# A fused two-block transformer kernel on one core: first group by sequences, last group by halves, and two biases moved from VectorE to TensorE

## The chip, the cores and the metric

The kernel runs on one core of a Trainium2 chip. The time is the device time of one launch in microseconds (us), the median of several runs. TensorE (PE) multiplies matrices into banks of the accumulation memory (2 KB for each of 128 partitions, so 512 float32 columns); VectorE (DVE) and ScalarE (ACT) read those banks, GpSimd (POOL) works on SBUF only, and SyncE (SP) issues the transfers. PEld is the loading of TensorE's weights.

## The reference

The input is 8 sequences of 256 tokens with 128 channels. Four parts follow each other, each with a residual and a layer norm behind it:

```python
# 1: linear attention: a decaying state for each of 16 heads of 8 channels
k = sigmoid(x @ key_w.T + key_b);  v, q = split(x @ vq_w.T)
kv = scan over t of (state * k + (1 - k) * v)            # 8 x 8 per head
x = layernorm(x + einsum(q, kv) @ out_w.T + out_b)
# 2: one of 8 linear maps, chosen by an argmax over noisy logits
x = layernorm(x + x @ W[idx] + b[idx])
# 3: attention without softmax through a symmetric metric per head
x = layernorm(x + nudged(x) @ mixer_w.T + mixer_b)
# 4: gated MLP, width 512, two more hidden layers with gelu
h = silu(x @ w1.T * s1) * (x @ w2.T * s2)
h = gelu(h @ h1.T * h1s);  h = gelu(h @ h2.T * h2s)
x = layernorm(x + h @ w3.T * s3)
```

## The kernel before, in words

The 8 sequences are handled in 4 groups (`NG`) of 2, so a group is `T` = 512 tokens, four tiles of 128 (`NT`). All groups run as one software pipeline: while group 2 is in part 1, group 1 is in part 3 and group 0 in part 4. There is no scheduler at run time. Each engine has a list of calls written out by hand (`without_weights` and `with_weights` for TensorE, plain lists for the others), executes it strictly in that order, and waits on semaphores where a call needs another engine's result. So what stands ahead of a call in its list matters as much as what it waits for.

*Part 1 of a group `a`.* `project(n)` makes key, value and query (three 512-column matmuls in float32). ScalarE moves them out (`projected`). VectorE takes the differences of the values (`value_steps`), ScalarE rounds them to the fast format fp32r (`high_values`, "high"), VectorE computes what the rounding lost (`low_values`, "low"), and `replicate(a, e)`, with e from 0 to 7, spreads them over the partitions with the matrix `rep_r`, which `cast_rows` makes at the start from a constant of the `heads` pack. VectorE then scans (`scan(a, e)`, two instructions of 256 columns), multiplies with the query (`read_state`), and TensorE applies the output weights (`attend(a, e)`).

*Parts 2 and 3.* `transposes(b, n)` turns the normed tiles, ScalarE moves them to SBUF (`move_x1`, `move_x2`, `high_x3`), `routed` multiplies with the chosen map plus identity into bank b4; `heads_of`, `gram_of`, `mix`, `through_metric` and `metric_out` do part 3 in b4 and b5. A norm is five calls: `norm_sum` adds the bias or residual and writes SBUF, `norm_stats`, `norm_moments` and `norm_varied` follow on VectorE, GpSimd raises the variance to the power -1/2 (`inverse_std`), and `norm_out` scales four tiles. For parts 2 and 3 `norm_sum` adds `chosen_b` or `mixer_b`.

*Part 4.* `gate_of` and `up_of`, two hidden layers (`hidden(c, layer, m)`, 8 matmuls each, high and low parts by the same fp32r weights), `narrow(c)` and `turn_back(c)`. ScalarE computes each gelu twice, rounded (`high_gelu`) and whole (`whole_gelu`); GpSimd or VectorE subtracts the two (`low_gelu`). `with_weights` begins once a flag has been computed and read by a branch.

## Time and profile before

| what | value |
|---|---|
| median of 3 runs (lowest, highest) | 204.92 us (204.56, 205.01) |
| the profiled execution's own time | 203.15 us |
| its span | 201.4 us |
| PE busy, instructions | 177.6 us (88%), 940 |
| DVE busy | 149.0 us (74%), 388 |
| ACT busy | 117.4 us (58%) |
| POOL busy | 68.4 us (34%) |
| mean granted TensorE clock | 0.989 |

The span is the part of the execution that the profiler sees; 1.75 us of the profiled execution lie around it. The profiled execution is 0.9% below the median of the runs shown. A row counts an engine as busy while an instruction is in it, so neighbouring instructions overlap a little; the distance between two starts says more about what one costs in a stream.

### The profile page before, as it was taken

Reading aid. Unit: us, or ns where it says so; the run is one execution under the profiler, and the core shown is the slowest. Engines: PE = TensorE matmul, PEld = TensorE weight load, DVE = VectorE, ACT = ScalarE, POOL = GpSimd, SP = SyncE. Lnnn points to the kernel's source line nnn. Section 1 sums busy time; section 2 is a strip of 40 time slices with the busy share of each in tenths; the row PEclk is TensorE's granted clock in tenths of the full one; section 3 lists DMA queues with packets and bytes.
Section 4 is the critical chain, followed back from the end, with each engine's and each line's share of the span. In section 5 each row is a group of like instructions: output and inputs, shape, how many; then the busy total and the mean of one; then the engine's idle time right before and its main releaser. Section 6 shows DMA issues by size and latency. Waiting matters only on the chain.

```text
span 201.4 us, 2831 instructions
## 1 busy us (share of the span) xinstructions
PE 177.6 (88%) x940; PEld 137.7 (68%) x940; DVE 149.0 (74%) x388; ACT 117.4 (58%) x178; POOL 68.4 (34%) x60
## 2 busy tenths in 40 slices
PE   7886878788976999999999999999899899999930
PEld 7245566466864887998789889866678677586810
DVE  0299999999999999999999955756772255753143
ACT  2698544095501785525577753498786459975720
POOL 4020002402012335343705545152549670554401
PEclk9999999999999999999999999999999999999995
DMA  5995002100000000010000000000001010000101
GB/s 144 333 433 215 3 0 80 52 0 0 3 0 0 3 3 0 0 52 3 0 2 0 3 0 0 0 0 3 0 0 37 19 52 3 2 0 1 51 3 55
DMA packets 6273, 7.83 MB, mean 39 GB/s; under 512 B 497, under 2 KB 5105, under 8 KB 6001
## 3 DMA queue, kind: packets, MB, share of 16 engines
q1 hardware_dynamic: 6256, 7.63, 11.1%
q8 instruction: 9, 0.15, 0.3%
q14 instruction: 8, 0.06, 0.1%
HBM read 6.58 MB, written 1.05 MB: 38 GB/s over the span
## 4 chain that ended last, share of the span: by engine, by line
PE 54%; DVE 23%; issue 10%; ACT 7%; DMA 2%; POOL 2%; POOLq 1%; DVEq 0%; SPq 0%; ACTq 0%
PE c_bank L1199 30%; DVE state L731 8%; PE y_bank L1106 7%; PE b_bank L1134 4%; PE b_bank L1129 3%; DVE read L741 3%; DMA heads_pack<-heads 2%; DVE stats L774 2%; PE rep_bank L1094 2%; PE b_bank L1199 2%; PE sum_bank L1199 2%; PE b_bank L1160 1%; DVE normed_lent L759 1%; DVE normed_lent L801 1%; ACT hid_even_high L482 1%
## 5 line engine op out<-in xcount | busy, mean ns | idle before, releaser
L731 DVE TENSOR_TENSOR_SCAN state<-rep_bank,keep 128x256 f32<-128x256 f32 x64 | 40.4, 675 | 2.3 <-PE rep_bank L1094 2.1
L1106 PEld LDWEIGHTS y_bank<-attend_pack,read 128*128 128x128 f32 x256 | 31.9, 191 | 8.2 <-DVE read L741 4.7
L1106 PE MATMUL y_bank<-attend_pack,read 128*128 128x128 f32 x256 | 33.6, 277 | 3.2 <-DVE total L766 1.9
L292 POOL TENSOR_TENSOR rstd<-varied,power 128x4 f32<-128x4 f32 x16 | 18.5, 1158 | 42.9 <-DVE varied L788 42.8
L741 DVE TENSOR_TENSOR read<-state,query 128x512 f32<-128x512 f32 x32 | 23.0, 730 | 0.5
L301 POOL TENSOR_TENSOR hid_odd_low<-hid,hid_odd_high 128x512 fp32r<-128x512 f32 x12 | 16.3, 1364 | 16.7 <-ACT hid L493 16.7
L493 ACT ACTIVATE hid<-c_bank,scales_pack 128x512 f32<-128x512 f32 x32 | 21.6, 683 | 0.0
L487 ACT ACTIVATE hid_even_high<-c_bank,scales_pack 128x512 fp32r<-128x512 f32 x16 | 11.0, 688 | 17.5 <-PE c_bank L1199 17.3
L1199 PE MATMUL c_bank<-hid_even_high,hidden_rounded 128*128 128x512 f32 x64 | 19.4, 410 | 1.0 <-ACT hid_even_high L482 0.8
L1199 PE MATMUL c_bank<-hid_odd_high,hidden_rounded 128*128 128x512 f32 x64 | 19.1, 410 | 0.0
L1199 PE MATMUL c_bank<-hid_odd_low,hidden_rounded 128*128 128x512 f32 x64 | 18.5, 398 | 0.4 <-DVE hid_odd_low L835 0.4
L1199 PE MATMUL c_bank<-hid_even_low,hidden_rounded 128*128 128x512 f32 x64 | 18.7, 400 | 0.0
L296 POOL TENSOR_TENSOR hid_even_low<-hid,hid_even_high 128x512 fp32r<-128x512 f32 x8 | 10.7, 1357 | 21.6 <-ACT hid_even_high L482 21.6
L301 POOL TENSOR_TENSOR hid_even_low<-hid,hid_even_high 128x512 fp32r<-128x512 f32 x8 | 10.8, 1355 | 16.3 <-ACT hid L493 16.3
L487 ACT ACTIVATE hid_odd_high<-c_bank,scales_pack 128x512 fp32r<-128x512 f32 x16 | 11.0, 688 | 8.2 <-PE c_bank L1199 8.1
L1199 PEld LDWEIGHTS c_bank<-hid_even_high,hidden_rounded 128*128 128x128 f32 x64 | 11.5, 189 | 4.6 <-ACT hid_even_high L482 1.7
L1199 PEld LDWEIGHTS c_bank<-hid_odd_low,hidden_rounded 128*128 128x128 f32 x64 | 12.0, 187 | 3.9 <-DVE hid_odd_low L835 0.7
L1199 PEld LDWEIGHTS c_bank<-hid_even_low,hidden_rounded 128*128 128x128 f32 x64 | 12.0, 188 | 3.7 <-DVE hid_even_low L830 1.1
L1071 PE MATMUL c_bank<-xT_lent,project_pack 128*128 128x512 f32 x24 | 12.7, 621 | 0.8 <-ACT keep L392 0.6
L1199 PEld LDWEIGHTS c_bank<-hid_odd_high,hidden_rounded 128*128 128x128 f32 x64 | 11.6, 190 | 2.2
L482 ACT CAST hid_even_high<-hid 128x512 fp32r<-128x512 f32 x16 | 9.9, 618 | 2.7 <-DVE hid L825 2.5
L801 DVE TENSOR_SCALAR normed_lent<-normed_lent,moments,rstd 128x128 f32<-128x128 f32 x32 | 8.9, 340 | 3.5 <-POOL rstd L292 3.4
(133 smaller groups left out, 336.6 us busy)
## 6 DMA issues: line engine op xcount, KB each, us to landing
hidden_pack<-hidden SPq DMA_DIRECT2D x2, 1024.0 KB, 11.0
xT_lent<-x_chan SPq DMA_DIRECT2D x4, 256.0 KB, 5.7
xt<-x_tok SPq DMA_DIRECT2D x4, 256.0 KB, 2.8
mlp_pack<-mlp SPq DMA_DIRECT2D x1, 768.0 KB, 8.0
out<-xT_lent SPq DMA_DIRECT2D x3, 256.0 KB, 2.3
attend_pack<-attend SPq DMA_DIRECT2D x1, 640.0 KB, 5.1
metric_pack<-metric SPq DMA_DIRECT2D x1, 448.0 KB, 12.5
out<-xT_lent SPq DMA_DIRECT2D x2, 128.0 KB, 1.8
```

What stands on the lines that cost most here:

```text
L292: nc.gpsimd.tensor_tensor(rstd[n][:], varied[n][:], power[:], ALU.pow).then_inc(ln_rstd[n], 1)
L296: nc.gpsimd.tensor_tensor(hid_parts[0][1][:, m, :], hid[:, m, :], hid_parts[0][0][:, m, :].bitcast(F32), ALU.subtract).then_inc(low_pool[0 ...
L301: nc.gpsimd.tensor_tensor(hid_parts[layer][1][:, m, :], hid[:, m, :], hid_parts[layer][0][:, m, :].bitcast(F32), ALU.subtract).then_inc(lo ...
L482: nc.scalar.copy(hid_parts[0][0][:, m, :], hid[:, m, :]).then_inc(product_high, 1)
L487: nc.scalar.activation(hid_parts[layer][0][:, m, :], c_bank[m % 2][:], ACT.Gelu, scale=scale).then_inc(gelu_high, 1)
L493: nc.scalar.activation(hid[:, m, :], c_bank[m % 2][:], ACT.Gelu, scale=scale).then_inc(gelu_done, 1)
L731: ins = nc.vector.tensor_tensor_scan(state[:, e % STATES, at], rep_bank[e % 2][:, at], keep[:, a * T + s * SEQ:a * T + (s + 1) * SEQ], 0.0 ...
L741: nc.vector.tensor_tensor(read[:, e % READS, :], state[:, e % STATES, :], query[:, a * T:(a + 1) * T], ALU.mult).then_inc(read_ready, 1)
L801: nc.vector.tensor_scalar(normed[n][:, tile(j)], total[n][:, tile(j)], moments[n][:, j, 0:1], rstd[n][:, j:j + 1], ALU.subtract, ALU.mult) ...
L1071: nc.tensor.matmul(proj_bank[n % 2][:], (key_w_sb, value_w_sb, query_w_sb)[k], xT[:, g * T:(g + 1) * T], start=True, stop=True).then_inc(p ...
L1106: ins = nc.tensor.matmul(y1_bank[:, tile(j)], read[:, e % READS, tile(j)], out_w_rep_sb[:, e, :], start=(e == 0 and j == 0), stop=False, s ...
L1199: return nc.tensor.matmul(bank_[:], weights[exact[0]][k], moving, start=(k == 0 and i == 0), stop=(k == last and i == 1))
```

## The change

Four things are done together.

1. *First group by sequences.* The packs `project` and `heads` are cut in four, the first 256 columns of the channel-major input come on their own, and three more transfers stand ahead of the input of groups 1 to 3. The first group's value and key projections, value differences, high and low parts and the first scan run for each sequence of 256 columns apart (`first_*`). Only 2 of the 8 slices of `rep_r` are cast at first. The warm-up is 6 matmuls instead of 8.
2. *Biases by TensorE.* `with_bias` puts behind each of the four tile products of `routed` and `metric_out` a second matmul into the same columns: a constant of 1/32 (64 x 128) times the bias in high and low part (64 x 128, fp32r). `norm_sum` is gone for parts 2 and 3, and their norms read bank b5 directly, `norm_stats` and `norm_out` alike. So `routed` goes from b4 to b5, and the small products between change banks too; `up_of(c, 0)`, which writes b5, now waits for `norm_out` of part 3 and no longer for its `norm_sum`.
3. *Last group's end by halves.* The last gelu, low part, `narrow`, scaling, turning back and norm of group 3 are done for tokens 0 to 255 and 256 to 511 apart (`*_last`, `narrow_early`, `narrow_late`).
4. *Other orders.* The lists of all engines are in a new order throughout.

```diff
-    ("project", (("key_w", P), ("value_w", P), ("query_w", P), ("key_b", 1))),
-    ("heads", (("rows_of", HD * HEADS), ("head_sum", P))),
+    ("values", (("value_w", P),)),
+    ("keys", (("key_w", P), ("query_w", P), ("key_b", 1))),
+    ("rows", (("rows_of", HD * HEADS),)),
+    ("sums", (("head_sum", P),)),
...
+        total[1] = total[2] = b5_bank
...
-            load_pack("project")
-            for g in range(NG):
+            load_pack("values")
+            sp.dma_start(xT[:, 0:SEQ], x_chan[:, 0:SEQ]).then_inc(x0_loaded, 16)
+            load_pack("keys")
+            sp.dma_start(xT[:, SEQ:T], x_chan[:, SEQ:T]).then_inc(xT_loaded[0], 16)
+            load_pack("rows")
+            load_pack("scales")
+            load_pack("sums")
+            load_pack("attend")
+            for g in range(1, NG):
                 at = slice(g * T, (g + 1) * T)
                 sp.dma_start(xT[:, at], x_chan[:, at]).then_inc(xT_loaded[g], 16)
-                if g == 0:
-                    load_pack("heads")
-                    load_pack("scales")
-                    load_pack("attend")
...
+            def cast_rows(i):
+                n = (0, 2, HD)[i], (0, 2, HD)[i + 1]
+                act.wait_ge(loaded["rows"], 16)
+                nc.scalar.copy(rep_r[:, n[0]:n[1], :].rearrange("p e (h d) -> p e h d", h=HEADS),
+                               rows_of_sb[:, n[0]:n[1], :].unsqueeze(3).to_broadcast([P, n[1] - n[0], HEADS, HD])
+                               ).then_inc(rep_cast, 1)
+
+            def first_value(s):
+                act.wait_ge(first["proj"], 2 * s + 1)
+                act.wait_ge(const_ready, 3)
+                nc.scalar.copy(value[:, s, 1:SEQ + 1], proj_bank[s][:, 0:SEQ]).then_inc(first["out"], 1)
+
+            def first_keep(s):
+                act.wait_ge(first["proj"], 2 * s + 2)
+                act.wait_ge(loaded["keys"], 16)
+                nc.scalar.activation(keep[:, s * SEQ:(s + 1) * SEQ], (b4_bank, b5_bank)[s][:, 0:SEQ], ACT.Sigmoid,
+                                     bias=key_b_sb).then_inc(first["out"], 1)
+
+            def first_query():
+                act.wait_ge(proj_ready, 1)
+                nc.scalar.copy(query[:, 0:T], y1_bank[:]).then_inc(proj_out, PROJECTIONS)
+
+            def first_high(s):
+                act.wait_ge(*((first["steps"], 1), (dv_whole, 1))[s])
+                nc.scalar.copy(dvalue_parts[0][0][half(0), s * SEQ:(s + 1) * SEQ],
+                               dvalue[half(0), s * SEQ:(s + 1) * SEQ]).then_inc((first["high"], dv_high)[s], 1)
...
+            def high_bias(n):
+                if n == 0:
+                    act.wait_ge(const_ready, 1)
+                    ins = nc.scalar.activation(thirty_seconds[:], ones[0:P // 2, :], ACT.Copy, scale=1.0 / 32.0)
+                elif n == 1:
+                    act.wait_ge(loaded["metric"], 16)
+                    ins = nc.scalar.copy(bias_parts[1][:], mixer_b_sb[0:P // 2, :])
+                else:
+                    act.wait_ge(chosen_loaded, 32)
+                    ins = nc.scalar.copy(bias_parts[0][:], chosen_b[0:P // 2, :])
+                ins.then_inc(bias_high, 1)
...
+            def high_gelu_last(i):
+                act.wait_ge(hidden_ready, 2 * NH * NG)
+                at = slice(i * T // 2, (i + 1) * T // 2)
+                nc.scalar.activation(hid_parts[2][0][:, NH - 1, at], c_bank[1][:, at], ACT.Gelu,
+                                     scale=h2s_sb[:, NH - 1:NH]).then_inc(last["gelu_high"], 1)
+
+            def whole_gelu_last(i):
+                act.wait_ge(hidden_ready, 2 * NH * NG)
+                at = slice(i * T // 2, (i + 1) * T // 2)
+                nc.scalar.activation(hid[:, NH - 1, at], c_bank[1][:, at], ACT.Gelu,
+                                     scale=h2s_sb[:, NH - 1:NH]).then_inc(last["gelu"], 1)
+
+            def narrow_out_last(i):
+                act.wait_ge(last["narrow"], i + 1)
+                nc.scalar.activation(narrowed[:, i * T // 2:(i + 1) * T // 2], (c_bank[0], rep_bank[0])[i][:, 0:T // 2],
+                                     ACT.Copy, scale=s3_sb[:, 0:1]).then_inc(last["narrow_out"], 1)
...
+            def first_steps(s):
+                dve.wait_ge(first["out"], 2 * s + 1)
+                nc.vector.tensor_tensor(dvalue[:, s * SEQ:(s + 1) * SEQ], value[:, s, 0:SEQ], value[:, s, 1:SEQ + 1],
+                                        ALU.subtract).then_inc((first["steps"], dv_whole)[s], 1)
+
+            def first_low(s):
+                dve.wait_ge(*((first["high"], 1), (dv_high, 1))[s])
+                at, parts = slice(s * SEQ, (s + 1) * SEQ), dvalue_parts[0][0]
+                nc.vector.tensor_tensor(parts[half(1), at], dvalue[half(0), at], parts[half(0), at].bitcast(F32),
+                                        ALU.subtract).then_inc((first["low"], dv_ready)[s], 1)
+
+            def first_scan(s):
+                dve.wait_ge(*((first["rep"], 1), (rep_ready, 1))[s])
+                dve.wait_ge(first["out"], 2 * s + 2)
+                at = slice(s * SEQ, (s + 1) * SEQ)
+                nc.vector.tensor_tensor_scan(state[:, 0, at], (sum_bank, rep_bank[0])[s][:, at], keep[:, at], 0.0, ALU.add,
+                                             ALU.mult).then_inc((first["scan"], scan_done)[s], 1)
...
-                if n in (1, 2):
-
-                    dve.wait_ge((routed_ready, metric_ready)[n - 1], g + 1)
-                    if n == 1 and g == 0:
-                        dve.wait_ge(chosen_loaded, 32)
-                    view = "p (j c) -> p j c"
-                    nc.vector.tensor_tensor(total[n].rearrange(view, j=NT),
-                                            (b4_bank, b5_bank)[n - 1][:].rearrange(view, j=NT),
-                                            (chosen_b[:], mixer_b_sb)[n - 1].unsqueeze(1).to_broadcast([P, NT, P]),
-                                            ALU.add).then_inc(ln_sum[n], 1)
-                else:
-                    dve.wait_ge(y1_ready if n == 0 else turned_back, g + 1)
-                    dve.wait_ge(res_ready[n], g + 1)
-                    nc.vector.tensor_tensor(total[n][:], y1_bank[:], (res0 if n == 0 else res3)[:],
-                                            ALU.add).then_inc(ln_sum[n], 1)
+                dve.wait_ge(y1_ready if n == 0 else turned_back, g + 1)
+                dve.wait_ge(res_ready[n], g + 1)
+                nc.vector.tensor_tensor(total[n][:], y1_bank[:], (res0 if n == 0 else res3)[:],
+                                        ALU.add).then_inc(ln_sum[n], 1)
 
             def norm_stats(n, g):
                 if g > 0:
                     dve.wait_ge(ln_moments[n], g)
-                dve.wait_ge(ln_sum[n], g + 1)
+
+                dve.wait_ge((ln_sum[0], routed_ready, metric_ready, ln_sum[3])[n], g + 1)
...
+            low_gelu(3, 2, 2)
+            low_gelu_last(0)
             norm_out(3, 2)
-            low_gelu(3, 2, 2)
-            low_gelu(3, 2, 3)
-            norm_sum(3, 3)
-            norm_stats(3, 3)
-            norm_moments(3, 3)
-            norm_varied(3, 3)
-            norm_out(3, 3)
+            low_gelu_last(1)
+            norm_sum_last(0)
+            norm_stats_last(0)
+            norm_moments_last(0)
+            norm_varied_last(0)
+            norm_sum_last(1)
+            norm_stats_last(1)
+            norm_moments_last(1)
+            norm_varied_last(1)
+            norm_out_last(0)
+            norm_out_last(1)
 
...
+            def first_project(k, s):
+                pe.wait_ge(loaded[("values", "keys")[k]], 16)
+                pe.wait_ge((x0_loaded, xT_loaded[0])[s], 16)
+                bank_ = proj_bank[s] if k == 0 else (b4_bank, b5_bank)[s]
+                nc.tensor.matmul(bank_[:, 0:SEQ], (value_w_sb, key_w_sb)[k], xT[:, s * SEQ:(s + 1) * SEQ], start=True,
+                                 stop=True).then_inc(first["proj"], 1)
+
+            def first_project_query():
+                pe.wait_ge(loaded["keys"], 16)
+                pe.wait_ge(x0_loaded, 16)
+                pe.wait_ge(xT_loaded[0], 16)
+                nc.tensor.matmul(y1_bank[:], query_w_sb, xT[:, 0:T], start=True, stop=True).then_inc(proj_ready, 1)
+
+            def first_replicate(s):
+                pe.wait_ge(*((first["low"], 1), (dv_ready, 1))[s])
+                pe.wait_ge(rep_cast, 1)
+                at = slice(s * SEQ, (s + 1) * SEQ)
+                nc.tensor.matmul((sum_bank, rep_bank[0])[s][:, at], rep_r[:, 0, :], dvalue_parts[0][0][:, at], start=True,
+                                 stop=True).then_inc((first["rep"], rep_ready)[s], 1)
...
+            def with_bias(src, w, bias):
+                for j in range(NT):
+                    nc.tensor.matmul(b5_bank[:, tile(j)], src[:, tile(j)], w(j), start=True, stop=False)
+                    ins = nc.tensor.matmul(b5_bank[:, tile(j)], thirty_seconds[:], bias[:], start=False, stop=True)
+                return ins
...
-                per_tile(b4_bank, x1T, lambda j: passed_w[:]).then_inc(routed_ready, 1)
-
-            def project_metric():
-                pe.wait_ge(loaded["metric"], 16)
-                nc.tensor.matmul(b5_bank[:, 0:P], metric_sb, proj_t_sb, start=True, stop=True).then_inc(pm_ready, 1)
-
-            def heads_of(b):
-                pe.wait_ge(x2_moved, b + 1)
                 if b == 0:
                     pe.wait_ge(pm_copied, 1)
                 else:
 
                     pe.wait_ge(product_done, NH * (b - 1) + 3)
+                with_bias(x1T, lambda j: passed_w[:], bias_parts[0]).then_inc(routed_ready, 1)
...
+                        ins = nc.tensor.matmul(b4_bank[:, tile(s)], heads[:, at], heads[:, at],
...
-                per_tile(b5_bank, x2T, lambda j: through[:, j // TPS, :]).then_inc(metric_ready, 1)
+                pe.wait_ge(mixed_moved, b + 1)
+                with_bias(x2T, lambda j: through[:, j // TPS, :], bias_parts[1]).then_inc(metric_ready, 1)
...
-                narrow(3)
-                turn_back(3)
+                narrow_early(0)
+                narrow_late(0)
+                narrow_early(1)
+                turn_back_last(0)
+                narrow_late(1)
+                turn_back_last(1)```

The start of ScalarE's list, first before, then after (the names are those of tiles; a number behind L is a line).

```order
2 L377 ACTIVATE spare<-ones 128x1 [waits const_ready]
3 L384 CAST rep_r<-heads_pack 128x1024 [waits heads_loaded]
4 L392 ACTIVATE keep<-c_bank,project_pack 128x512 [waits project_loaded,proj_ready]
5 L395 COPY value<-c_bank 128x2x256 [waits const_ready,proj_ready]
6 L406 CAST dvalue_first<-dvalue 64x512 [waits dv_whole]
```

```order
2 L398 ACTIVATE spare<-ones 128x1 [waits const_ready]
3 L406 CAST rep_r<-rows_pack 128x256 [waits rows_loaded]
4 L413 COPY value<-c_bank 128x256 [waits const_ready,first_proj]
5 L418 ACTIVATE keep<-b_bank,keys_pack 128x256 [waits keys_loaded,first_proj]
6 L413 COPY value<-c_bank 128x256 [waits const_ready,first_proj]
7 L427 CAST dvalue_first<-dvalue 64x256 [waits first_steps]
```

The cast of `rep_r` still stands first, but has a quarter of its columns; the value comes ahead of the key, by 256 columns.

TensorE's list around the branch that starts `with_weights`, before and after, with the numbers of the banks.

```order
60 L1094 MATMUL rep_bank0<-dvalue_first0,rep_r 128x512
61 L1106 MATMUL y1_bank<-attend_pack,read 128x128 x4
62 L1129 MATMUL b4_bank<-metric_pack,normed_lent 128x128 x4
63 L1094 MATMUL rep_bank1<-dvalue_first0,rep_r 128x512
64 L1485 TENSOR_LOAD fits_flag
```

```order
78 L1262 MATMUL rep_bank1<-dvalue_first0,rep_r 128x512
79 L1262 MATMUL rep_bank0<-dvalue_second0,rep_r 128x512
80 L1275 MATMUL y1_bank<-attend_pack,read 128x128 x4
81 L1299 MATMUL b4_bank<-metric_pack,normed_lent 128x128 x4
82 L1275 MATMUL y1_bank<-attend_pack,read 128x128 x4
83 L1713 TENSOR_LOAD fits_flag
```

One `replicate` (the fifth of group 2) and one `attend` more now stand ahead of the branch.

The end of VectorE's list after the change; before, `norm_out(3, 2)` stood ahead of the last two `low_gelu`, and the five calls of the last norm followed once, for 512 columns.

```order
277 L897 TENSOR_TENSOR hid_even_low<-hid,hid_even_high 128x256 [waits last_gelu]
278 L891 TENSOR_SCALAR xT_lent<-xT_lent,moments,rstd 128x128 [waits stored,ln3_rstd]
279 L891 TENSOR_SCALAR xT_lent<-xT_lent,moments,rstd 128x128 x3
280 L897 TENSOR_TENSOR hid_even_low<-hid,hid_even_high 128x256 [waits last_gelu]
281 L905 TENSOR_TENSOR xT_lent<-y_bank,res 128x256 [waits ln3_out,res3_ready,last_turned]
```

Four scalings of group 2 (numbers 278 and 279) now stand between the two halves of the last low part.

## Rows read from the trace of the kernel before

**Rows 1.** Windows: busy us and count of each engine, TensorE's clock, DMA share, GB/s.

```profile
12.37:64.65 52.28, 41.78 (x244) 30.43 (x244) 51.10 (x126) 25.36 (x37) 6.04 (x7) 1.00 0.15 56
64.65:129.00 64.35, 64.35 (x390) 55.80 (x391) 58.09 (x142) 36.37 (x58) 27.54 (x20) 1.00 0.02 5
129.00:193.02 64.02, 60.83 (x276) 45.09 (x274) 32.87 (x100) 48.17 (x74) 30.73 (x26) 1.00 0.04 13
```

**Rows 2.** Timeline of the start: start, us, engine, line, operation, idle before.

```profile
6.07 1.04 ACT L384 CAST rep_r<-heads_pack 128x1024 fp32r<-128x1024 f32 x1 [3.83 <-DMA heads_pack<-heads]
...
7.02 0.68 ACT L392 ACTIVATE keep<-c_bank,project_pack 128x512 f32<-128x512 f32 x1
7.60 0.58 ACT L395 COPY value<-c_bank 128x512 f32<-128x512 f32 x1
...
8.28 0.69 DVE L707 TENSOR_TENSOR dvalue<-value 128x512 f32<-128x512 f32 x1 [1.58 <-ACT value L395]
...
11.10 1.27 DVE L731 TENSOR_TENSOR_SCAN state<-rep_bank,keep 128x256 f32<-128x256 f32 x2
```

**Rows 3.** Timeline around the branch, VectorE and TensorE.

```profile
62.21 1.26 DVE L731 TENSOR_TENSOR_SCAN state<-rep_bank,keep 128x256 f32<-128x256 f32 x2
...
63.53 0.49 PE L1094 MATMUL rep_bank<-dvalue_first,rep_r 128*128 128x512 f32 x1 [0.91 <-DVE state L731]
64.65 0.47 PE L1199 MATMUL sum_bank<-x3T_high,mlp_rounded 128*128 128x512 f32 x1 [0.63 <-issue]
```

**Rows 4.** Chain that ended last: start us, us in the chain, what.

```profile
69.28 0.44 PE b_bank L1129 x4
...
71.07 0.89 PE b_bank L1134 x8
...
73.09 5.69 PE c_bank L1199 x24
```

**Rows 5.** Groups by form: busy us, mean ns; operations of VectorE and ScalarE.

```profile
L816 DVE TENSOR_TENSOR x3T_low<-b_bank,x3T_high 128x512 fp32r<-128x512 f32 x4 | 2.7, 682 | 1.0 <-ACT x3T_high L462 1.0
L835 DVE TENSOR_TENSOR hid_odd_low<-hid,hid_odd_high 128x512 fp32r<-128x512 f32 x4 | 2.8, 689 | 4.2 <-ACT hid L493 4.2
...
L455 ACT COPY mixed<-b_bank 128x256 f32<-128x256 f32 x4 | 1.5, 372 | 5.4 <-PE b_bank L1168 5.4
```

**Rows 6.** Chain that ended last, part 3's norm of group 3.

```profile
162.11 0.70 DVE normed_lent L759
...
164.55 1.02 POOL rstd L292
...
166.08 1.01 PE b_bank L1129 x4
```

**Rows 7.** Who waited for whom, TensorE, 64 to 192 us: total, times, longest.

```profile
PE c_bank L1199 <- ACT hid_even_high L482: 0.8, 2, 0.7
PE b_bank L1129 <- DVE normed_lent L801: 0.7, 2, 0.4
```

**Rows 8.** Timeline of the end.

```profile
190.46 0.69 ACT L487 ACTIVATE hid_even_high<-c_bank,scales_pack 128x512 fp32r<-128x512 f32 x1 [0.60 <-PE c_bank L1199]
...
192.50 0.50 PE L1199 MATMUL c_bank<-hid_even_low,mlp_rounded 128*128 128x512 f32 x1 [0.45 <-DVE hid_even_low L835]
193.03 0.69 ACT L497 ACTIVATE gate<-c_bank,scales_pack 128x512 f32<-128x512 f32 x1 [1.31 <-PE c_bank L1199]
...
193.77 0.66 PE L1278 MATMUL y_bank<-metric_pack,gate 128*128 128x128 f32 x4 [0.78 <-ACT gate L497]
194.53 0.69 DVE L766 TENSOR_TENSOR xT_lent<-y_bank,res 128x512 f32<-128x512 f32 x1 [2.08 <-PE y_bank L1278]
195.32 0.87 DVE L774 BATCH_NORM_STATS2 stats<-xT_lent 128x6 f32<-128x128 f32 x4
...
196.96 1.01 POOL L292 TENSOR_TENSOR rstd<-varied,power 128x4 f32<-128x4 f32 x1 [7.61 <-DVE varied L788]
198.00 1.11 DVE L801 TENSOR_SCALAR xT_lent<-xT_lent,moments,rstd 128x128 f32<-128x128 f32 x4 [1.12 <-POOL rstd L292]
```

More of the change, by code:

```diff
@@ L179, in build @@
         proj_ready, proj_out = sem("proj_ready"), sem("proj_out")
+        first = {name: sem("first_" + name) for name in ("proj", "out", "steps", "high", "low", "rep", "scan")}
+        last = {name: sem("last_" + name) for name in ("gelu_high", "gelu", "low", "narrow", "narrow_out", "turned", "sum",
+                                                       "stats", "moments", "varied", "rstd")}
         dv_whole, dv_high, dv_ready = sem("dv_whole"), sem("dv_high"), sem("dv_ready")
@@ L957, in _ @@
-            norm_sum(2, 1)
             norm_stats(2, 1)
@@ L1076, in sum_query @@
                 if a == 0:
-                    pe.wait_ge(loaded["heads"], 16)
+                    pe.wait_ge(loaded["sums"], 16)
+                    pe.wait_ge(first["scan"], 1)
                 else:
```

627 lines of the change are left out of this document (367 added, 260 removed).

## The prediction, made before the changed kernel was run

> **What bounds the kernel now.** I read the busy time by stretch first, then the chain that ended last, and the timeline where the chain changes engine. They give four stretches. To 12 us the kernel fills its pipeline. From 12.37 to 64.65 us VectorE is busy 51.1 of 52.3 us while TensorE has 10.5 us idle: VectorE's list sets the pace [rows 1]. The chain turns to TensorE at the branch: VectorE ends a scan at 63.47, the `replicate` that waited for it starts at 63.53, and the first product of part 4 at 64.65, with 0.63 us of branching ahead of it [rows 3]. From there to 129 us TensorE has no gap at all, and to 193.02 it idles 3.2 of 64.0 us [rows 1]. So there each matmul added or taken away counts in full. The last stretch is a serial hand-over from engine to engine, from the last gelu (190.46) to the last scaling (ends 199.11), with 2.3 us behind it for the store [rows 8].
>
> **The change, part by part.** Sums are made against the profiled execution (203.15 us); the median of the runs shown is 0.9% above it, and I scale at the end.
>
> *Start.* ScalarE waited until 6.07 us for the `heads` pack, cast 1024 columns in 1.04 us, then made the key and only then the value, which reached VectorE at 8.28; the first scan began at 11.10 [rows 2] and its second half ended at 12.37. After the change the pack of the rows is the fifth transfer, but the bytes up to and with it (columns of the packs and of the input, 512 bytes each) are 512 KB and were 576 KB, so I let it land at the same 6.1. A 256-column pass of ScalarE took 0.37 [rows 5]: cast to 6.5, value to 6.9, difference on VectorE (0.4, somewhat over half of 0.69) to 7.3. ScalarE meanwhile does key, second value and then the high part to 8.1; low part 8.5, `replicate` of 256 columns 8.9, first scan 9.6, `low_values(0, 1)` 10.3, second scan 10.95. That is 1.4 us earlier; with a dozen hand-overs I take 1.2, bounds 0.5 (the pack lands later, behind three more issues) and 1.8. Three more issues also shift SP's queue by some 1.3 us: group 1's input, tokens and MLP weights come later, but the first reader of each still stands behind VectorE's backlog. If that cover fails, the start's gain is what it costs. The warm-up's two missing matmuls cost nothing: TensorE waits for input then.
>
> *To the branch.* The new last item before it is `attend(2, 1)`, which needs `read_state(2, 1)`. Against the old point (the scan's end at 63.47) VectorE's list has more: one pair of scans, 1.26; one read, 0.69; two `low_bias`, 0.4 (128 columns, 0.22 each by the statistics [rows 8]). It has less: two `norm_sum` of parts 2 and 3, 1.4 at 0.70 [rows 6]; one `norm_stats`, 0.87 [rows 8], and one `direct_product`, 0.69 by rows of that shape [rows 5], which now follow. Net 0.6 less, with the start 1.8: VectorE is there at 61.7, `attend` takes 0.89, hand-over and branch 0.7, so 63.3 instead of 64.65. And TensorE has one `replicate` (0.49, [rows 3]) and one `attend` (0.89, as eight records of that size take in [rows 4]) behind it already, 1.4 more. Together 2.7; I take **-2.5**, since VectorE's own 1.2 us of gaps may grow. Bounds -0.5 and -3.5.
>
> *The bias matmuls.* 32 are added, 24 of them (six calls in groups 1 to 3) where TensorE is the bound. No row shows an fp32r matmul of 128 columns. The nearest: single-record matmuls of 128 columns (the transposes) stand 0.11 apart; the float32 product of that shape costs 0.22 (eight records, 0.89); an fp32r product of 512 columns costs 0.237 (5.69 for 24), a quarter of which is 0.06 [rows 4]. The weight load would hold the last one up, as it does in the transposes, so I take 0.11: **+2.7**, bounds +1.4 and +5.3. The eight calls of before the branch lie in TensorE's idle time there.
>
> *The norms from the bank.* On the chain part 3's norm of group 3 runs from 162.11 to 166.08, where the transposes start; 0.70 of it is `norm_sum` [rows 6]. TensorE has two hidden products to cover it and runs short; waits of this kind and idle around them make 0.7 us by the waits' own sum [rows 7] and part of the 3.2 us. A norm shorter by 0.7 stays under cover in groups 2 and 3: **-1.0**, bounds 0 and -2. What is late next there is ScalarE's rounding of the product (0.8 [rows 7]), which the change does not touch. Bank as source is no dearer in the trace: 682 ns against 689 from SBUF for the same shape [rows 5]. The statistics and scalings from a bank have no row; I take them as unchanged. The Trainium skill speaks against this (VectorE: DVE Perf Modes, "Why PSUM operands drop a tier"): a float32 operation with one source may run at double rate from SBUF but never from a bank. By that page's clock it would cost an estimated 0.07 us for each scaling of 128 columns, 0.27 a norm, and no row here shows such a scaling. The same mechanism, priced from rows, is a rival below. The later release for `up_of(c, 0)` costs nothing: the same norm must end before there is an x3 to multiply.
>
> *The end.* From 190.46: four gelu passes of 256 columns end at 190.85, 191.2, 191.5 and 191.9; low part 0 at 191.65, its last two matmuls 192.0, scaling 192.4. TensorE then does six 256-column matmuls of half 1 (192.7) and turns half 0 back (193.0). Half 1's low part stands behind `norm_out(3, 2)`, 1.11 as the same shape takes [rows 8]: 193.15 instead of 192.3; matmuls 193.5, scaling 193.9, turned 194.2. VectorE sums and measures half 0 to 194.4 and half 1 to 195.6; GpSimd's power took 1.01 for four columns [rows 8] and I keep that for two, to 196.7; the last two scalings end at 197.3 against 199.11. That is 1.8, and with eight hand-overs of 0.05 **-1.4**, bounds -0.7 and -2.0. The third store must have landed before half 0 is scaled; it starts near 193.4 and has until 195.6. Splitting six calls into narrower ones adds **+0.1**.
>
> *Sum.* -2.5 + 2.7 - 1.0 - 1.4 + 0.1 = -2.1: 201.05 us for a profiled execution, and times 204.92/203.15, **202.8 us**.
>
> **The rivals.**
> - *The narrow fp32r matmul is dear* (the side of slower). At 0.22, the price of the float32 product, six calls on TensorE's path cost 5.3: 203.15 + 0.5 = 203.7, or 205.5. It decides from about 0.19 us each on. For it: nothing in the trace shows that fp32r keeps its rate at 128 columns. Against: fp32r needs one record where float32 needs two. 17%.
> - *Scaling from the bank is slow.* A column costs VectorE 1.2 ns (0.69 for a sum of 512 less 0.22 for statistics of 128, over 384 [rows 8]); if half of 128 is lost, 0.3 a norm comes back on VectorE and on the norm's chain: two norms before the branch, 0.6, and 0.4 of cover, so 203.8. For it: no row of such a scaling. Against: [rows 5]. 10%.
> - *The start's gain does not arrive.* A pack late by a microsecond, or one of VectorE's new neighbours waiting, and only -0.5 of the 2.5 is left: 204.8 to 205.3. For it: VectorE has 1.2 us of slack in 52 [rows 1], so one badly placed wait shows at once. 13%.
> - *The orders fit better still.* TensorE's 3.2 us of idle time mostly gone and the bias at 0.06: 200.5 to 201.5. 12%.
> - The forecast, 202.0 to 203.8: 48%.
>
> **Numbers.** Forecast, good order and slow scaling are all faster (70%); a change within 0.2% (0.4 us, about what this kernel's runs can tell from none) comes from the third rival's near half and the edge of the first, 11%; slower 19%. The range reaches from the good orders to the dear matmul, 200.8 to 205.4.
>
> **What would show it.** In the changed profile: the first scan near 9.0 us; the first product of part 4 near 63.3 with one `attend` more behind it; bias matmuls 0.11 apart from their neighbours, a call of `routed` 1.3 us long and not 0.9 or 1.8; statistics at 0.22 and scalings at 0.28 distance from b5; no TensorE wait ahead of part 3's transposes; the last scaling's end 7.2 us behind the start of the last gelu and not 8.65. Wrong would make it: gaps on TensorE between 64 and 129 us, where there are none now, or a bias call near 1.8 us.

## Result and profile of the changed kernel

The changed kernel took **213.72 us** (median of four runs, 213.29 to 214.48) where the kernel before, on the same chip, took 204.96 (204.56 to 205.15): a ratio of **1.0434, interval 1.0399 to 1.0469**. Forecast were 202.8 us and a range up to 205.4. The change makes the kernel slower by 4%, outside the range and the other way from what was forecast. Runs of the kernel before fall into two groups: around 203.0 us at a mean granted clock of 0.985 to 0.99, as its profile (203.15 us), and around 204.6 us near 0.98, as the four runs here by their times. A few slow runs are left out of the ratios and medians below.

The profiled execution took 213.29 us, its span 211.5. I cut it at the marks of the prediction (times are those of the profiled executions; the last column reaches from the end of the last scaling to the execution's own time):

| kernel | first scan | first product of part 4 | from there to the last gelu | last gelu to last scaling's end | behind it |
|---|---|---|---|---|---|
| before | 11.10 | 64.65 | 125.81 | 8.65 | 4.04 |
| after | 8.25 | 64.83 | 135.90 | 7.02 | 5.54 |

The medians are 8.76 us apart, the two profiles 10.14. This difference is +0.18 to the branch, **+10.09** between it and the last gelu, -1.63 in the hand-over at the end, +1.50 behind the last scaling. The middle stretch in windows, from the first product of part 4 to the last gelu, of before and of after (columns as in [rows 1]):

```profile
64.65:190.46 125.81, 123.08 (x657) 99.77 (x658) 90.15 (x241) 83.28 (x130) 58.26 (x46) 1.00 0.03 9
```

```profile
64.83:200.73 135.90, 132.93 (x674) 104.34 (x674) 87.95 (x235) 84.38 (x132) 56.27 (x46) 1.00 0.02 7
```

TensorE idles 2.7 us in the one and 3.0 in the other, at the full clock in both. So waits don't make the +10.1: TensorE is *busy* 9.9 us longer. The timeline of TensorE in after, one call of `metric_out` with its eight matmuls (start, us, line, operation), shows on what:

```profile
134.79 0.39 PE L1309 MATMUL b_bank<-through,x1T 128*128 128x128 f32 x2
135.11 0.32 PE L1310 MATMUL b_bank<-bias_parts,thirty_seconds 64*128 64x128 f32 x1
135.36 0.49 PE L1309 MATMUL b_bank<-through,x1T 128*128 128x128 f32 x2
135.78 0.33 PE L1310 MATMUL b_bank<-bias_parts,thirty_seconds 64*128 64x128 f32 x1
...
137.12 0.32 PE L1310 MATMUL b_bank<-bias_parts,thirty_seconds 64*128 64x128 f32 x1
137.38 1.16 PE L1275 MATMUL y_bank<-attend_pack,read 128*128 128x128 f32 x8
```

A bias matmul has 64 rows of weights, a product 128; I call this number the height of the weights. From one bias matmul to the next it is 0.67 us, where a product alone has 0.22 (0.89 for the call of four in [rows 4]). A bias matmul costs 0.45 us, not 0.11, and only 0.25 of it (135.11 to 135.36) passes before the next product starts: the product behind it is dearer as well, 0.42 to the next bias matmul instead of 0.22. The forecast named a call of 1.8 us as the sign of being wrong; this one takes 2.59 (134.79 to 137.38). The weight loads of the same stretch show what goes with it:

```profile
135.11 0.18 PEld L1310 LDWEIGHTS b_bank<-bias_parts,thirty_seconds 64*128 64x128 f32 x1
135.36 0.30 PEld L1309 LDWEIGHTS b_bank<-through,x1T 128*128 128x128 f32 x2
135.78 0.18 PEld L1310 LDWEIGHTS b_bank<-bias_parts,thirty_seconds 64*128 64x128 f32 x1
```

Each load starts in the same hundredth as its own matmul. It isn't done under the matmul before it, and that at both changes of height, from 128 to 64 and back.

The start, in the timeline of after (compare [rows 2]):

```profile
5.28 0.40 ACT L406 CAST rep_r<-rows_pack 128x256 fp32r<-128x256 f32 x1 [3.04 <-DMA rows_pack<-rows]
...
6.04 0.42 DVE L783 TENSOR_TENSOR dvalue<-value 128x256 f32<-128x256 f32 x1 [6.04 <-ACT value L413]
...
8.25 0.69 DVE L796 TENSOR_TENSOR_SCAN state<-sum_bank,keep 128x256 f32<-128x256 f32 x1
```

The first scan is 2.85 us earlier, twice the forecast (7.71 to 8.72 us in the profiles of the variants with this start). The pack landed at 5.28 and not at 6.1, and from the end of the first high part (7.16) to the scan it took 1.09 us where I had counted 1.5. Up to 36 us stands a wait longer than any that TensorE has in the kernel before (1.8 us at most from 12 to 64 us), on GpSimd's and TensorE's timelines:

```profile
34.07 0.46 POOL L301 TENSOR_TENSOR passed_w<-chosen_w,metric_pack 128x128 f32<-128x128 f32 x1 [19.47 <-DMA chosen_b<-ffn_b]
34.48 1.02 POOL L307 TENSOR_TENSOR rstd<-varied,power 128x4 f32<-128x4 f32 x1
...
36.04 1.15 PE L1299 MATMUL b_bank<-metric_pack,normed 128*128 128x128 f32 x4 [3.40 <-DVE normed L891]
```

GpSimd's list has the chosen weights, which come with a late DMA, ahead of the first norm's power. TensorE stands 3.40 us for that norm, and its clock falls behind the wait (third column from the end, 30 to 40 us and 40 to 50 us):

```profile
30.00:40.00 10.00, 6.43 (x24) 4.09 (x24) 9.27 (x28) 4.25 (x8) 1.44 (x2) 0.83 0.13 39
40.00:50.00 10.00, 9.89 (x55) 7.13 (x56) 7.90 (x23) 2.27 (x5) 2.62 (x2) 1.00 0.09 26
```

From 40 us on TensorE is busy 9.89 of 10 us *ahead* of the branch. The eight bias matmuls of group 0, which I had put at nothing, lie between 39 and 59 us. The end, against [rows 8]:

```profile
200.73 0.47 ACT L552 ACTIVATE hid_even_high<-c_bank,scales_pack 128x256 fp32r<-128x256 f32 x1 [0.60 <-PE c_bank L1382]
...
205.01 0.70 POOL L336 TENSOR_TENSOR rstd<-varied,power 128x2 f32<-128x2 f32 x1 [5.02 <-DVE varied L926]
...
206.85 1.31 SPq L274 DMA_DIRECT2D out<-xT_lent  x2
207.15 0.60 DVE L933 TENSOR_SCALAR xT_lent<-xT_lent,moments,rstd 128x128 f32<-128x128 f32 x2 [0.33 <-POOL rstd L336]
```

Here the forecast of 7.2 us is met to 0.2: 7.02 from gelu to scaling. The power takes 0.70 for two columns, not 1.01, so without that luck it would have been 7.3.

### The profile page after: what moved, and what is told of

It reads as the page before. It is cut to its first block, busy times and chain, and to the rows that moved or that the text cites. A ratio compares the mean times of both kernels' runs of the same rounds, so it can differ in the third digit from the quotient of the medians.

```text
span 211.5 us, 2947 instructions
## 1 busy us (share of the span) xinstructions
PE 191.5 (91%) x981; PEld 146.9 (69%) x981; DVE 147.4 (70%) x387; ACT 118.4 (56%) x188; POOL 64.5 (31%) x61
## 3 DMA queue, kind: packets, MB, share of 16 engines
q1 hardware_dynamic: 6688, 7.63, 10.9%
HBM read 6.58 MB, written 1.05 MB: 36 GB/s over the span
## 4 chain that ended last, share of the span: by engine, by line
PE 71%; DVE 10%; issue 5%; ACT 4%; DMA 3%; SPq 2%; POOL 1%; POOLq 0%; DVEq 0%
PE c_bank L1382 32%; PE y_bank L1275 9%; PE b_bank L1309 6%; PE b_bank L1299 4%; PE b_bank L1310 4%; DVE state L831 3%; DMA xT_lent<-x_chan 3%; PE c_bank L1236 2%; PE rep_bank L1262 2%; PE b_bank L1382 2%; PE b_bank L1341 2%; PE b_bank L1304 2%; PE sum_bank L1382 2%; PE y_bank L1282 1%; DVE read L841 1%
## 5 line engine op out<-in xcount | busy, mean ns | idle before, releaser
L831 DVE TENSOR_TENSOR_SCAN state<-rep_bank,keep 128x256 f32<-128x256 f32 x62 | 38.9, 673 | 1.6 <-PE rep_bank L1262 1.6
L1275 PEld LDWEIGHTS y_bank<-attend_pack,read 128*128 128x128 f32 x256 | 31.9, 191 | 6.6 <-DVE read L841 3.3
L1275 PE MATMUL y_bank<-attend_pack,read 128*128 128x128 f32 x256 | 34.4, 279 | 1.2 <-DVE read L841 0.6
L307 POOL TENSOR_TENSOR rstd<-varied,power 128x4 f32<-128x4 f32 x15 | 15.9, 1060 | 56.9 <-DVE varied L878 56.8
L841 DVE TENSOR_TENSOR read<-state,query 128x512 f32<-128x512 f32 x32 | 22.6, 714 | 0.1
L541 ACT ACTIVATE hid_even_high<-c_bank,scales_pack 128x512 fp32r<-128x512 f32 x15 | 10.3, 689 | 16.9 <-PE c_bank L1382 16.8
L316 POOL TENSOR_TENSOR hid_odd_low<-hid,hid_odd_high 128x512 fp32r<-128x512 f32 x12 | 16.0, 1339 | 11.7 <-ACT hid L547 11.6
L1382 PE MATMUL c_bank<-hid_even_high,hidden_rounded 128*128 128x512 f32 x64 | 19.1, 410 | 0.3 <-ACT gate L530 0.3
L1382 PE MATMUL c_bank<-hid_odd_high,hidden_rounded 128*128 128x512 f32 x64 | 19.2, 411 | 0.0
L1382 PE MATMUL c_bank<-hid_odd_low,hidden_rounded 128*128 128x512 f32 x64 | 18.4, 397 | 0.5 <-DVE hid_odd_low L975 0.5
L1382 PE MATMUL c_bank<-hid_even_low,hidden_rounded 128*128 128x512 f32 x64 | 18.5, 398 | 0.0
L316 POOL TENSOR_TENSOR hid_even_low<-hid,hid_even_high 128x512 fp32r<-128x512 f32 x8 | 10.6, 1330 | 20.5 <-ACT hid L547 20.5
L864 DVE BATCH_NORM_STATS2 stats<-b_bank 128x6 f32<-128x128 f32 x32 | 7.1, 285 | 13.8 <-PE b_bank L1310 13.8
L1382 PEld LDWEIGHTS c_bank<-hid_odd_low,hidden_rounded 128*128 128x128 f32 x64 | 12.0, 188 | 3.8 <-DVE hid_odd_low L975 0.9
L1382 PEld LDWEIGHTS c_bank<-hid_even_low,hidden_rounded 128*128 128x128 f32 x64 | 12.0, 188 | 3.4 <-DVE hid_even_low L970 0.7
L311 POOL TENSOR_TENSOR hid_even_low<-hid,hid_even_high 128x512 fp32r<-128x512 f32 x8 | 10.4, 1323 | 12.5 <-ACT hid_even_high L536 12.5
L1382 PEld LDWEIGHTS c_bank<-hid_even_high,hidden_rounded 128*128 128x128 f32 x64 | 11.4, 189 | 3.4 <-ACT gate L530 0.7
L1382 PEld LDWEIGHTS c_bank<-hid_odd_high,hidden_rounded 128*128 128x128 f32 x64 | 11.5, 189 | 2.2
L891 DVE TENSOR_SCALAR normed_lent<-b_bank,moments,rstd 128x128 f32<-128x128 f32 x32 | 10.9, 403 | 2.7 <-POOL rstd L307 2.7
```

The lines of the kernel that those rows point to most:

```text
L307: nc.gpsimd.tensor_tensor(rstd[n][:], varied[n][:], power[:], ALU.pow).then_inc(ln_rstd[n], 1)
L311: nc.gpsimd.tensor_tensor(hid_parts[0][1][:, m, :], hid[:, m, :], hid_parts[0][0][:, m, :].bitcast(F32), ALU.subtract).then_inc(low_pool[0 ...
L316: nc.gpsimd.tensor_tensor(hid_parts[layer][1][:, m, :], hid[:, m, :], hid_parts[layer][0][:, m, :].bitcast(F32), ALU.subtract).then_inc(lo ...
L541: nc.scalar.activation(hid_parts[layer][0][:, m, :], c_bank[m % 2][:], ACT.Gelu, scale=scale).then_inc(gelu_high, 1)
L831: ins = nc.vector.tensor_tensor_scan(state[:, e % STATES, at], rep_bank[e % 2][:, at], keep[:, a * T + s * SEQ:a * T + (s + 1) * SEQ], 0.0 ...
L841: nc.vector.tensor_tensor(read[:, e % READS, :], state[:, e % STATES, :], query[:, a * T:(a + 1) * T], ALU.mult).then_inc(read_ready, 1)
```

## The experiments

All ratios are to the kernel before, run beside the variants on the same chip; its median there was 203.42 us for the a runs, 203.89 for b and c, 203.20 for d. The ratio need not be the quotient of the medians. Between runs with different letters the ratios say more than the times.

**a1: the changed kernel without the bias matmuls.** It leaves the biases of parts 2 and 3 out.

```diff
-                nc.tensor.matmul(b5_bank[:, tile(j)], src[:, tile(j)], w(j), start=True, stop=False)
-                ins = nc.tensor.matmul(b5_bank[:, tile(j)], thirty_seconds[:], bias[:], start=False, stop=True)
+                ins = nc.tensor.matmul(b5_bank[:, tile(j)], src[:, tile(j)], w(j), start=True, stop=True)
```

> The changed kernel with the 32 bias matmuls left out (so the biases of parts 2 and 3 are left out of the result). In the changed kernel a tile of a call with bias takes 0.67 us where the product alone took 0.22, so 0.45 more, 24 times on TensorE's path, and the operation behind each call another 0.2. If these matmuls are the cause of the loss, about 11 to 12 us go: 202 us. If the loss lies in the new orders or in the early stall at 33 us, it stays above 210.

Measured: 205.17 us, 1.0076 (1.0043 to 1.0108), not the 202 expected. The matmuls carry most of the loss: 3.6 of the 4.3% by the ratios, or 8.5 of the 8.8 us by the medians. But without them the kernel is still no faster than before, where my sum without its +2.7 gave -4.8.

**a2: the bias over 128 rows instead of 64.**

```diff
-        bias_parts = [sb(f"bias_parts{n}", [P // 2, P], F32R) for n in (1, 2)]
-        thirty_seconds = sb("thirty_seconds", [P // 2, P], F32R)
+        bias_parts = [sb(f"bias_parts{n}", [P, P], F32R) for n in (1, 2)]
+        thirty_seconds = sb("thirty_seconds", [P, P], F32R)
```

(with 1/64 in place of 1/32 and the low parts in rows 64 to 127).

> The changed kernel with bias matmuls over 128 rows instead of 64 (constant 1/64, bias high and low in 64 rows each); same count, same columns, same format. Theory S (the switch between 64 and 128 rows keeps weights from being loaded behind the running matmul): the tile falls from 0.67 to about 0.33, the loss shrinks by 8 us: 205 to 206 us. Rival N (an fp32r matmul of 128 columns is slow by itself, whatever its rows): no change, 213 to 214 us.

Measured: 205.43 us, 1.0109 (1.0037 to 1.0182). As many matmuls of as many columns, only the height of the weights changed, and 8.3 us are gone by the medians, 7.9 between the two profiles, 6.6 by the ratios. TensorE's timeline of a2:

```profile
91.51 0.30 PE L1310 MATMUL b_bank<-bias_parts,thirty_seconds 128*128 128x128 f32 x1
91.60 0.30 PEld L1309 LDWEIGHTS b_bank<-through,x1T 128*128 128x128 f32 x2
91.66 0.44 PE L1309 MATMUL b_bank<-through,x1T 128*128 128x128 f32 x2
...
91.85 0.31 PE L1310 MATMUL b_bank<-bias_parts,thirty_seconds 128*128 128x128 f32 x1
```

The period is 0.34 us, so 0.12 for a bias matmul, and the next product's load (91.60) starts under the running matmul (91.51 to 91.81). The windows from the branch to the last gelu agree, of a1 and of a2:

```profile
62.93:191.72 128.79, 122.97 (x650) 97.97 (x650) 88.60 (x235) 84.71 (x132) 56.13 (x46) 1.00 0.02 7
```

```profile
62.60:192.68 130.08, 125.55 (x674) 100.78 (x674) 88.62 (x235) 84.61 (x131) 56.10 (x46) 1.00 0.03 7
```

24 bias matmuls add (125.55 - 122.97) / 24 = **0.11 us** each over 128 rows, my price to the digit, and (132.93 - 122.97) / 24 = **0.42** each over 64. The Trainium skill (TensorE: Matmul & The Clock Gate, "Part 3: Packing small matmuls — row/col tiling") says that a weight load overlaps a running matmul only where their row groups (strips of 32 rows) differ; earlier in the same section it also lets a load go ahead into a background weight buffer. The loads over all 128 rows here do overlap (91.60 under 91.51 to 91.81), against the first statement and in line with the second. The loads at a change of height, 64 rows beside 128, don't.

**a3: one 64-row bias matmul of 512 columns ahead of the four products.**

```diff
+                nc.tensor.matmul(b5_bank[:].rearrange("p (j c) -> p j c", j=NT), thirty_seconds[:],
+                                 bias[:].unsqueeze(1).to_broadcast([bias.shape[0], NT, P]), start=True, stop=False)
                 for j in range(NT):
-                    nc.tensor.matmul(b5_bank[:, tile(j)], src[:, tile(j)], w(j), start=True, stop=False)
-                    ins = nc.tensor.matmul(b5_bank[:, tile(j)], thirty_seconds[:], bias[:], start=False, stop=True)
+                    ins = nc.tensor.matmul(b5_bank[:, tile(j)], src[:, tile(j)], w(j), start=False, stop=(j == NT - 1))
```

> The changed kernel with one 512-column bias matmul (64 rows, the bias repeated four times by its access pattern) ahead of the four products of a call instead of four of 128 columns. Theory S: one switch in and out instead of four, a call takes about 0.89 + 0.24 + 0.4 = 1.5 instead of 2.67: 7 us less, 206 to 207 us. Rival N: 0.24 for the wide one and nothing else, 1.13 a call: 9 us less, 204 to 205 us.

Measured: 207.42 us, 1.0152 (1.0076 to 1.0227). Two changes of height in a call instead of eight:

```profile
111.86 0.50 PE L1308 MATMUL b_bank<-bias_parts,thirty_seconds 64*128 64x512 f32 x1
112.29 1.16 PE L1311 MATMUL b_bank<-passed_w,x1T 128*128 128x128 f32 x8
...
113.28 0.39 PE L1275 MATMUL y_bank<-attend_pack,read 128*128 128x128 f32 x2
```

A call takes 1.42 us (111.86 to 113.28), 2.59 in after. Its wide matmul takes 0.43 us to the next start and its products 0.99; over 128 rows (d1 below) they take 0.32 and 0.89. So one pair of changes costs 0.2 us here, and 0.3 around each 128-column matmul in after. That it is the change of height that is dear and not a 64-row matmul by itself is my reading and not shown: a3 has fewer of both, and no variant has two 64-row matmuls in a row.

**a4: part 2 undone in the new orders.** VectorE adds the biases again, in eight `norm_sum`.

> The changed kernel with part 2 undone: VectorE adds the biases from bank b5 into SBUF in a norm_sum again (0.7 us each, 8 times), no bias matmuls; all orders, the start and the end as changed. If the bias matmuls are the whole loss: 202 to 203.5 us, at or under the kernel before (205). If the new orders cost by themselves: above 205.

Measured: 214.72 us, 1.0544 (1.0471 to 1.0617). TensorE's waits from 64 to 192 us of a4, and the same one in a1:

```profile
PE b_bank L1312 <- DVE normed_lent L898: 6.9, 8, 2.1
```

```profile
PE b_bank L1299 <- DVE normed_lent L891: 1.3, 1, 1.3
```

The new orders can't carry VectorE's eight sums; this variant also keeps the one bank and the later release of the change. Part of its time goes with the granted clock, 0.74 in 30 to 40 us and 0.94 in 100 to 130 (a1: 0.89 and 1.00). So the parts of the change aren't additive: in these orders part 2 is worth up to 9.6 us (a1 against a4), which a good form of it brings and the 64-row form spends again.

**b1: the kernel before with the end by halves alone.**

> The kernel before with part 3 alone: the end of group 3 by halves, all other lists as before. In the changed kernel the last scaling ends 7.0 us behind the start of the last gelu, before it was 8.65; but the span ran 3.75 us on behind it where it ran 2.3 before. Theory E (the tail gain is real, the late store is chance): 1.0 to 1.6 us less than before. Rival L (the later landing belongs to the halves, each store being issued on its own): 0 to 0.3 us less.

Measured: 203.14 us, 0.9978 (0.9939 to 1.0016). The hand-over took 7.02 us instead of 8.65, but 4.99 us lay behind the last scaling instead of 4.04. At the same granted clock b1 is 0.4 to 0.5 us shorter (median 202.49 against 202.95 at 0.985 to 0.99, 204.23 against 204.58 below), nearer to rival L than to theory E.

**b2 and b3: the kernel before with part 2 alone**, over 64 and over 128 rows, its other orders untouched.

> The kernel before with part 2 alone: biases by TensorE over 64 rows, norms of parts 2 and 3 straight from banks b4 and b5, old orders. A call costs TensorE 1.8 us more and the operation behind it 0.2; six calls on its path: 12 us more, less what shorter norms free (up to 1.5): 214 to 216 us. If the old orders hide it: under 210.

> As the run before, but over 128 rows. In the 128-row run in the new orders a bias matmul stood 0.15 from the next product and that took 0.19: 0.34 a tile instead of 0.22. Six calls of 0.48 more: +2.9, less 0.5 to 1.5 from shorter norms and VectorE's lighter list before the branch (two norm_sum, 1.3 us, less 0.35 for scalings from the bank): +0.3 to +2 us over before. Theory V (VectorE's time ahead of the branch is worth its full size): no more than +1. Rival T (TensorE's list alone decides): +2 or more.

Measured: 219.93 us, 1.0783 (1.0714 to 1.0852), and 207.38, 1.0161 (1.0095 to 1.0228). b2 is above its 214 to 216 us; b3, 3.3 us over by its ratio, is on rival T's side. The 64 rows cost 12.6 us more than the 128 here, 8.3 in the new orders. The first product of part 4 starts at 69.64 us in b2 and at 64.90 in b3, but that is not all the price of the eight bias matmuls ahead of it, 8 x 0.31 = 2.5 us. b2's granted clock was low there:

```profile
40.00:50.00 10.00, 9.23 (x28) 6.18 (x28) 7.77 (x23) 5.38 (x5) 1.49 (x1) 0.66 0.00 0
```

At 0.66 on average, 6.8 of these 10 us ran at the lower level of 1.2 GHz, during and behind the first bias call, which is up to 3.4 us of lost time; b3's clock was 1.00 in this window. So I take the difference between 12.6 and 8.3 as mostly the clock's. VectorE's relief brings b3 nothing by itself: in the old orders the branch stays where it was (64.65 before), and TensorE does the bias matmuls on top. Windows of b3, 64 to 100 us:

```profile
64.00:100.00 36.00, 35.35 (x198) 30.28 (x198) 31.77 (x75) 17.26 (x28) 14.32 (x11) 0.91 0.03 8
```

The granted clock was 0.91 there, at most 3.2 us of lost time in this profile. It is not the whole loss: the b3 run with a mean clock of 0.989, that of before's profile, took 206.72 us, where the kernel before takes 203.0 at that clock.

**c1: a2 with the first norm's power ahead of the chosen weights on GpSimd.**

```diff
-            passed_weights()
             inverse_std(0, 0)
+            passed_weights()
```

> The changed kernel with 128-row biases, and on GpSimd the first inverse_std ahead of passed_weights, which waits for the chosen weights. TensorE then stands 3.6 us at the first transposes until 36.6 us and its granted clock falls to 0.83 in 30 to 40 us. Theory Q (that stall is a queueing one and costs time): rstd comes 1.4 us earlier, the stall shrinks to about 2.2, and 0.5 to 1.5 us go against the 128-row run (205.4). Rival B (VectorE's backlog sets the pace there, the stall is cover): no change within 0.4 us.

Measured: 204.28 us, 1.0032 (0.9996 to 1.0068). The branch came at 61.12 us instead of 62.60, and the clock stayed up:

```profile
30.00:40.00 10.00, 6.66 (x35) 4.59 (x35) 9.81 (x30) 4.87 (x9) 1.45 (x2) 1.00 0.14 39
```

TensorE's wait ahead of the first transposes went from 3.6 to 2.8 us. But the later branch times with the same order are 61.73, 61.38 and 62.20 us (d1, d2, d3), so one profile doesn't fix the gain; by the medians it is 1.1 us (205.43 to 204.28), by the ratios 1.6, and the intervals overlap. d1, d2 and d3 also show the low clock again (0.83 to 0.85 in that window) with the same wait. The order shortens the wait; it doesn't pin the clock. Nor do c1's runs show that the clock costs time there: the profiled one, at a mean of 0.990, took 204.13 us, those at 0.983 to 0.984 took 203.80 to 204.63.

**d1, d2, d3: better forms on top of c1.** d1 makes a3's wide bias matmul over 128 rows; d2 moves `norm_out(3, 2)` and its power forward, ahead of group 3's last low parts; d3 moves one VectorE step:

```diff
             norm_out(1, 1)
+            low_values(3, 0)
             read_state(2, 6)
             scan(2, 7)
-            low_values(3, 0)
             scan(3, 0)
```

> The run with rstd first and 128-row biases, but each call's four 128-column bias matmuls are one of 512 columns ahead of the products. A bias matmul of 128 rows added 0.115 us, 0.46 a call; one of 512 columns should take 0.24. Theory S: no switch of rows, so 0.2 a call less on TensorE's path: 1 to 1.4 us under the run before it (204.3). If a wide matmul ahead of float32 products costs what it did over 64 rows (the products' first load not behind it): no gain or up to 1 us more.

> As d1, and group 2's last scaling (norm_out(3, 2)) and its inverse_std are back where they stood before the change, ahead of the last low parts, so that its store starts some 8 us earlier. In two of the profiles (a1, a3) VectorE waited 1.9 and 2.1 us for that store ahead of the last scalings. Theory W (the wait for the third store comes and goes with its landing time): the median falls by 0.5 to 1.5 us and the runs scatter less. Rival: the wait is rare, no change beyond 0.3 us.

> As d2, and VectorE computes the first low values of group 3 (low_values(3, 0)) ahead of read_state(2, 6) and scan(2, 7) instead of behind them. In the new orders TensorE waits 1.4 to 1.6 us there for them between 64 and 100 us, where it had no wait before. Theory O (this place in the new order is itself a loss): 0.8 to 1.5 us less. Rival: the wait moves to the next replicate or attend, within 0.4 us of d2.

Measured: d1 203.83 us, 0.9986 (0.9945 to 1.0027); d2 203.93, 1.0009 (0.9977 to 1.0040); d3 **202.60, 0.9936 (0.9899 to 0.9972)**. d1 is 0.5 us under c1 by the medians and 0.9 by the ratios, less than its theory S and within the noise. The wide matmul costs 0.32 us a call, not four times 0.11:

```profile
109.51 0.48 PE L1308 MATMUL b_bank<-bias_parts,thirty_seconds 128*128 128x512 f32 x1
109.83 1.05 PE L1311 MATMUL b_bank<-passed_w,x1T 128*128 128x128 f32 x8
...
110.72 0.39 PE L1275 MATMUL y_bank<-attend_pack,read 128*128 128x128 f32 x2
```

d2 was meant against a wait that a1, a3 and a4 show (1.9, 2.1 and 1.8 us) and the others don't. VectorE's last scaling in a1 waited for the third store, which took 5.0 us to land there and 2.3 in after:

```profile
199.17 1.12 DVE L933 TENSOR_SCALAR xT_lent<-xT_lent,moments,rstd 128x128 f32<-128x128 f32 x4 [1.88 <-DMA out<-xT_lent]
```

At the median that wait is worth nothing (d1 and d2 are equal), as the rival said. d3 removes a wait of TensorE for `low_values(3, 0)`, 1.2 to 1.6 us long in a1, a2, a3, c1, d1 and d2; here in a1:

```profile
PE rep_bank L1262 <- DVE dvalue_first L812: 1.6, 1, 1.6
```

After itself does not have it; I take it that the 64-row bias matmuls kept TensorE late enough. d3 is the only variant whose interval lies wholly below the kernel before, by 0.6%. It is the best of several, so its size is to be taken with the whole interval.

## Why the prediction was wrong

**The step that failed is "The bias matmuls".** I priced an fp32r matmul of 128 columns from rows in which all weights have 128 rows, and the bounds of 0.06 and 0.22 came from the same kind of row. I asked what its data type and its columns cost, and never that its weights have 64 rows between products with 128. The price is 0.11 us for the matmul over 128 rows, and 0.42 to 0.45 for the form of the change: +10.0 us of TensorE's time behind the branch instead of +2.7. Of these, 7.1 lengthen the stretch (135.90 against 128.79 in a1) and the rest fills idle time that a1 has. That the height is what costs is shown by a2 (height alone, -8.3 us by the medians), and a3 agrees (a quarter of the 64-row matmuls, -6.3). The rival "the narrow fp32r matmul is dear" named the right place and sign, but the wrong cause and half the price. That the eight ahead of the branch "lie in TensorE's idle time" failed with it: after's branch (64.83) is 2.2 us behind a2's (62.60) and 1.9 behind a1's.

**To the branch (-2.5).** Of this, 1.35 was to show as an earlier branch (63.3), and that much did: a1 stands there at 62.93 and a2 at 62.60, with the 3.4 to 3.6 us wait at 36 us still in them, and c1 at 61.12. In after the 64-row bias took it all back (64.83). The other part, 1.15, was work that TensorE should have had behind it at the branch, and the windows do not show it: a1's TensorE is busy 122.97 us behind the branch, before's 123.08. Part of it was a slip: I priced the `replicate` at the length of its record (0.49), where its like in a stream takes 0.24 to the next start. Added up from start to start, gaps left out, a1 has 0.94 us less of `attend` and `replicate` in this stretch, and 0.50 more for the same 344 products of part 4 and 0.29 more for the same 36 transposes. What the new order does to these is not shown.

**The norms from the bank (-1.0).** It did not come. In a1 TensorE idles 5.8 us from the branch to the last gelu (128.79 - 122.97), against 2.7 before. I had judged the waits at their old places; after the reordering they stand elsewhere (the two rows of a1 above). Removing one of them was worth 1.3 us at the median (d3 against d2). The slow scaling, a rival, is real and small. My argument against it, [rows 5], compared a subtraction with two sources; the scaling has one. Groups by form (columns as in [rows 5]), two of before from SBUF, then two of after from the bank:

```profile
L801 DVE TENSOR_SCALAR normed_lent<-normed_lent,moments,rstd 128x128 f32<-128x128 f32 x32 | 8.9, 340 | 3.5 <-POOL rstd L292 3.4
...
L774 DVE BATCH_NORM_STATS2 stats<-normed_lent 128x6 f32<-128x128 f32 x32 | 7.0, 281 | 0.6
```

```profile
L891 DVE TENSOR_SCALAR normed_lent<-b_bank,moments,rstd 128x128 f32<-128x128 f32 x32 | 10.9, 403 | 2.7 <-POOL rstd L307 2.7
...
L864 DVE BATCH_NORM_STATS2 stats<-b_bank 128x6 f32<-128x128 f32 x32 | 7.1, 285 | 13.8 <-PE b_bank L1310 13.8
```

The scaling is 0.06 us slower, 0.25 a norm; the statistics are no slower (285 against 281 ns). The Trainium skill (VectorE: DVE Perf Modes, "Why PSUM operands drop a tier") led to an estimate of 0.07 and 0.27, and the trace agrees.

**The end (-1.4).** Right in the hand-over: it takes 7.02 to 7.04 us in after, a2, b1, c1, d1, d2 and d3 alike, though 0.3 of it came from the shorter power, which I had not counted on. Mis-sized in what I left out: behind the last scaling before has 4.04 us and the kernels with halves have 4.99 to 6.17. In after the two stores at the end took 2.6 us to land by the median, 1.8 in before. b1 shows what is left, -0.2% with an interval that includes none. Why they land later stays open.

**The start** gave more than forecast, and the third store had landed in time in after.

**What is left of the sum.** Without the bias it was -4.8. a1's profile has +3.3 instead (206.45 against 203.15, and 1.3 of it above a1's own median). The 8.1 between them: -0.4 at the branch (62.93, not 63.3); +5.0 from there to the last gelu (+2.98, where attend's 1.15, the norms' 1.0 and the splitting made -2.05), 3.1 of it new idle time; +1.3 in the hand-over, through the wait for the store; +2.1 behind the last scaling. In after the same places are hidden under the 10.0 us of the bias, except the last.

## What to carry to other kernels

Price an instruction from a row that has its neighbour too: a 128-column matmul over 64 rows between products over 128 costs here four times what it costs over 128 rows, and padding the contraction to 128 rows cost nothing that a2 shows. A change that moves the bound from one engine to another needs its orders read again for the waits that the old bound hid; each is found in the new trace, not in the old one. And parts of such a change aren't additive: one may be needed by another (a4) and a loss alone (b3).

## What was unexpected of the hardware

- In after, a weight load of 64 rows is not done under a running matmul of 128 rows, nor the other way round: 0.42 us for each bias matmul in the window sums, 0.11 with 128 rows throughout (a2).
- A VectorE instruction that starts shortly after one of GpSimd took about 1.0 us longer. In the timeline of a2 (`read_state` takes 0.69 otherwise):

```profile
78.52 3.01 POOL L316 TENSOR_TENSOR hid_odd_low<-hid,hid_odd_high 128x512 fp32r<-128x512 f32 x2
78.62 1.74 DVE L841 TENSOR_TENSOR read<-state,query 128x512 f32<-128x512 f32 x1
```

The kernel before has it too, in fewer places. Whether it is the shared start was not tried.
- A 256 KB store landed 2.3 us after its issue by the median of each profile; the third store took 5.0 us in a1 and a4 and 5.2 in a3.
- The granted clock behind the same wait is not always the same: with TensorE idle for 2.8 us ahead of the first transposes it was 1.00 in 30 to 40 us in c1 and 0.83 in d1 and d2.
